# Experts chosen first, two of four routers as fp32 dots on VectorE, a softmax in two halves, and first outputs moved among the operand sums

## Chip, cores and metric

The kernel runs on one core of a Trainium2 chip. The metric is device time of one execution in microseconds, median of several runs.

## Reference, cut to what matters

```python
# x: [4, 512, 512]; layer 1: layernorm, an int8-quantised gated MLP per batch, residual
x = x + xattn(_layernorm(x), gate_up, ctx)
# layer 2, on the 2048 tokens xn = _layernorm(x):
logits = xn @ gate_w.T                            # gate_w: [8, 512]
_, sel = top_k(logits.sum(axis=0), 2)             # two experts for all tokens
rw = softmax(logits[:, sel], axis=1)              # a weight per token and expert
h = gelu(einsum('nd,kdf->knf', xn, w1[sel]) + b1[sel][:, None, :])
y = einsum('knf,kfd->knd', h, w2[sel]) + b2[sel][:, None, :]
out = x + einsum('nk,knd->nd', rw, y)
```

The same two experts serve all tokens. The softmax is over two logits only, so a weight depends on their difference alone.

## The kernel before, in words

It is a Bass program written by engine: each engine has a list of calls in its own order, and semaphores tie them together. PE is TensorE, DVE VectorE, ACT ScalarE, POOL GpSimd, SP the engine that issues the loads.

*Layer 1* (to about 140 us) runs the four batches b = 0 to 3 interleaved. *Layer 2* takes the two experts in 16 units of 256 hidden columns, 8 "pairs" of two halves: half tp = 0 has batches 0 and 1, tp = 1 batches 2 and 3. Every fp32 operand is split into a high part (rounded, made on ACT) and a low part (the rest, made by a subtraction), and a product is three matmuls: high x high, high x low, low x high. `keep_hi`/`keep_lo(b, h)` make those of the normalised, transposed tokens of batch b; `hid_lo` (POOL) those of the hidden h; `first_weights` and `first_down_weights` those of the first w1 and w2 (ACT high, DVE low).

The head of layer 2 is the stretch in question:
- `normed2(b, h)` on PE transposes normalised tokens (L656). DVE and ACT sum them over tokens (`token_sums`, `token_total`); `expert_sums` on PE (L677) turns the sums into eight expert totals; `choose_experts` on DVE finds the top two (L1349) and SP then loads w1, w2 and bias rows of the chosen experts.
- `router(b)` on PE (L667) makes the logits of 512 tokens for all 8 experts, 8 matmuls with 512 columns each. ACT copies them out, `logit_columns(b)` (L685) transposes them back, and `pick_logits` on DVE picks the columns of the chosen two. POOL raises e to the (negative) difference (L523), and `token_weights` on DVE makes the softmax weights (L1519 to L1523).
- `first_pair` differs from later pairs: `plain(q, n)` (L850) computes four tiles of a half, 12 matmuls each, with plain products; from pair 1 on `strassen` (L792) needs seven products of combined operands instead of eight. The sums of operands that this wants are made during the first pair: `last_operands`, `middle_operands`, `fourth_operand` (L1295, L1310), their high parts `operand_hi` on ACT, low parts `operand_lo` on DVE (L1316).
- `down` (L805) multiplies h by w2 into four PSUM banks of y. `outputs_of(p, tp, s)` on DVE (L1541) adds weight times y to the residual in SBUF and thereby frees each bank (`y_free`), which the block of downs after the next waits for. `bias_rows` (L1532) adds b2. In later pairs `combine` (L1570) sums products on DVE; the next product into the same bank waits for it (`comb_ready`).

The order around the change is the order of the calls in each engine's list. DVE's first pair before, in short:

```python
last_operands(0); fourth_operand(0); token_weights()
outputs_of(0, 0, 0); middle_operands(0, 3); middle_operands(0, 4); outputs_of(0, 0, 1)
operand_lo(0, 0..3); last_operands(1); fourth_operand(1)
bias_rows(0); outputs(0, 1)
```

Of the kernel before, what the change touches and what calls it, by code (L numbers as in the profile page):

```python
# [5 lines left out]
ALU = mybir.AluOpType  # L6
# [5 lines left out]
AX = mybir.AxisListType  # L12
ds = bass.ds

P = 128
# [8 lines left out]
def xattn_ffn(  # L24
# [21 lines left out]
    NT = B * TT  # L46
    FW = 2 * P
# [14 lines left out]
    with ExitStack() as ctx:  # L62
# [6 lines left out]
        def each(name):  # L69
# [42 lines left out]
        logits = sb("logits", [2 * E, B, T])  # L112
# [8 lines left out]
        lk = sb("lk", [P, TOPK, NT])  # L121
        lmin = sb("lmin", [P, NT])
        lmax = sb("lmax", [P, NT])
# [12 lines left out]


# [16 lines left out]
        rstd = [batch_sb(f"rstd{c}_", [P, TT]) for c in (1, 2)]  # L154
        nmean = [batch_sb(f"nmean{c}_", [P, TT]) for c in (1, 2)]
# [78 lines left out]
        raw1_load, raw2_load = sem("raw1_load"), sem("raw2_load")  # L234
        b1_load, b2_load = sem("b1_load"), sem("b2_load")
# [18 lines left out]
        def _(sp):  # L254
# [37 lines left out]
            load_w1(0)  # L292
# [25 lines left out]
        def _(pool):  # L318
# [200 lines left out]
            def first_pair():  # L519
                hid_lo(0, 0, 0)  # L520
                hid_lo(0, 0, 1)
                pool.wait_ge(lsub_ready, 1)
                g.tensor_tensor(lpow[:, :], euler[:, :], lsub[:, :], ALU.pow).then_inc(lexp_ready, 1)  # L523
                hid_lo(0, 0, 2)
                hid_lo(0, 0, 3)
                weight_sums(0)
                for i in range(4):
                    hid_lo(0, 1, i)
                for i in range(7):
                    weight_lo(0, i)  # L530
                down_lo(0, 0, 1)
                down_lo(0, 1, 0)

            first_pair()
# [6 lines left out]
        def _(pe):  # L541
# [139 lines left out]
            def logit_columns(b):  # L681
                emptied(f"r.{b}")
# [156 lines left out]
            def plain(q, n):  # L839
# [3 lines left out]
                for h in range(KD // H):  # L843
                    if q == 0:
                        pe.wait_ge(a_ops_ready, 2 * f + h + 1)
# [780 lines left out]
```

## Time and profile before

| what | value |
|---|---|
| time, median of 3 runs (lowest, highest) | 819.7 us (818.9, 820.05) |
| profiled execution, span from first to last instruction | 818.7 us |
| its own time as shown | the span alone is given for it; the median of the runs is 1.0 us above the span |
| PE busy | 771.5 us (94%) |
| DVE busy | 477.7 us (58%) |
| POOL busy | 449.7 us (55%) |
| ACT busy | 354.6 us (43%) |
| first tile of layer 2 (L850) on PE | from about 153.6 us on |

A busy PE says that its queue is full, not that its clock is: the granted clock is read apart. Shares over the whole span hide that DVE is much fuller in the first pair than later.

### The profile page before, as it was taken

Reading aid. Unit: us, or ns where it says so; the run is one execution under the profiler, and the core shown is the slowest. Engines: PE = TensorE matmul, PEld = TensorE weight load, DVE = VectorE, ACT = ScalarE, POOL = GpSimd, SP = SyncE. Lnnn points to the kernel's source line nnn. Section 1 sums busy time; section 2 is a strip of 40 time slices with the busy share of each in tenths; the row PEclk is TensorE's granted clock in tenths of the full one; section 3 lists DMA queues with packets and bytes.
Section 4 is the critical chain, followed back from the end, with each engine's and each line's share of the span. In section 5 each row is a group of like instructions: output and inputs, shape, how many; then the busy total and the mean of one; then the engine's idle time right before and its main releaser. Section 6 shows DMA issues by size and latency. Waiting matters only on the chain.

```text
span 818.7 us, 11342 instructions
## 1 busy us (share of the span) xinstructions
PE 771.5 (94%) x3570; PEld 624.1 (76%) x3577; DVE 477.7 (58%) x669; ACT 354.6 (43%) x660; POOL 449.7 (55%) x497
## 2 busy tenths in 40 slices
PE   5688666999999999999999999999999999999998
PEld 4666455688788888888888888888888888888886
DVE  5999759797754545454545454545454545454545
ACT  3967588743442434343424343434343434242422
POOL 1789997157564646464646464646464646464622
PEclk9899968999999999999999999999999999999999
DMA  9400000301010101010101010101010101010022
GB/s 344 173 2 1 1 0 2 129 1 51 1 52 1 51 0 49 3 50 2 48 4 51 1 45 6 42 9 44 7 41 11 36 15 36 15 32 19 0 103 104
DMA packets 19077, 32.34 MB, mean 39 GB/s; under 512 B 872, under 2 KB 11240, under 8 KB 18160
## 3 DMA queue, kind: packets, MB, share of 16 engines
q1 hardware_dynamic: 18896, 31.98, 11.1%
q8 instruction: 12, 0.20, 0.1%
q10 hardware_dynamic: 160, 0.08, 0.0%
q14 instruction: 9, 0.07, 0.0%
HBM read 27.87 MB, written 4.19 MB: 39 GB/s over the span
## 4 chain that ended last, share of the span: by engine, by line
PE 83%; POOL 8%; DVE 3%; issue 2%; ACT 2%; DMA 1%; ACTq 0%; POOLq 0%; DVEq 0%
PE slot L805 42%; PE slot L792 34%; PE slot L850 3%; POOL wv L366 2%; POOL xf L383 1%; PE slot L667 1%; POOL wv L372 1%; POOL cv L366 1%; PE slot L585 1%; DVE rmax L1226 1%; DMA b_rows<-in_L_ffn_b 1%; POOL rstd L340 1%; POOL h_lo L476 1%; DVE stats L1217 1%; DVE peak_x L1226 1%
## 5 line engine op out<-in xcount | busy, mean ns | idle before, releaser
L792 PE MATMUL slot<-xo,a_hi 128*128 128x512 f32 x840 | 259.1, 390 | 0.0
L1541 DVE SCALAR_TENSOR_TENSOR res<-slot,rw,res 128x512 f32<-128x512 f32 x256 | 178.5, 750 | 130.3 <-PE slot L805 130.2
L1570 DVE TENSOR_TENSOR e<-slot,e 128x512 f32<-128x512 f32 x150 | 103.8, 692 | 173.4 <-PE slot L792 173.3
L805 PE MATMUL slot<-w_hi,h_hi 128*128 128x512 f32 x512 | 201.3, 393 | 0.4 <-POOL h_lo L476 0.4
L805 PE MATMUL slot<-w_lo,h_hi 128*128 128x512 f32 x512 | 199.6, 390 | 0.0
L805 PE MATMUL slot<-w_hi,h_lo 128*128 128x512 f32 x512 | 199.4, 390 | 0.0
L792 PEld LDWEIGHTS slot<-xo,a_hi 128*128 128x128 f32 x840 | 157.4, 188 | 33.3 <-DVE e L1570 0.2
L476 POOL TENSOR_TENSOR h_lo<-e,h_hi 128x512 fp32r<-128x512 f32 x96 | 138.1, 1451 | 55.0 <-ACT e L1104 54.0
L792 PE MATMUL slot<-xo,a_lo 128*128 128x512 f32 x420 | 163.7, 390 | 0.0
L805 PEld LDWEIGHTS slot<-w_hi,h_hi 128*128 128x128 f32 x512 | 96.1, 188 | 25.1 <-POOL h_lo L476 5.6
L476 POOL TENSOR_TENSOR h_lo<-hid,h_hi 128x512 fp32r<-128x512 f32 x32 | 44.1, 1378 | 124.7 <-ACT hid L1104 124.7
L805 PEld LDWEIGHTS slot<-w_hi,h_lo 128*128 128x128 f32 x512 | 96.2, 188 | 20.1
L805 PEld LDWEIGHTS slot<-w_lo,h_hi 128*128 128x128 f32 x512 | 96.2, 188 | 19.3
L792 PEld LDWEIGHTS slot<-xo,a_lo 128*128 128x128 f32 x420 | 78.9, 188 | 16.5
L1103 ACT ACTIVATE h_hi<-e,b_now 128x512 fp32r<-128x512 f32 x90 | 64.9, 721 | 58.0 <-DVE e L1570 57.6
L1142 ACT COPY e<-slot 128x512 f32<-128x512 f32 x30 | 17.6, 587 | 164.5 <-PE slot L792 164.5
L490 POOL TENSOR_TENSOR a_lo<-raw,a_hi 128x256 fp32r<-128x256 f32 x45 | 34.3, 761 | 95.9 <-ACT a_hi L988 95.9
L991 ACT CAST w_hi<-raw 128x512 fp32r<-128x512 f32 x32 | 19.8, 622 | 109.8 <-PE slot L805 109.8
L495 POOL TENSOR_TENSOR w_lo<-raw,w_hi 128x512 fp32r<-128x512 f32 x30 | 38.7, 1289 | 50.4 <-ACT w_hi L991 50.4
L1104 ACT ACTIVATE e<-e,b_now 128x512 f32<-128x512 f32 x90 | 63.8, 709 | 0.0
L1103 ACT ACTIVATE h_hi<-slot,b_now 128x512 fp32r<-128x512 f32 x38 | 26.2, 689 | 66.5 <-PE slot L792 56.6
L490 POOL TENSOR_TENSOR a_lo<-ssum,a_hi 128x256 fp32r<-128x256 f32 x60 | 43.7, 739 | 0.0
(145 smaller groups left out, 814.5 us busy)
## 6 DMA issues: line engine op xcount, KB each, us to landing
raw<-in_L_ffn_w SPq DMA_DIRECT2D x32, 512.0 KB, 3.4
res<-in_x SPq DMA_DIRECT2D x4, 1024.0 KB, 11.9
wv<-in_fside_BxS2xS SPq DMA_DIRECT2D x4, 1024.0 KB, 12.8
out_x<-res SPq DMA_DIRECT2D x3, 1024.0 KB, 3.9
cv<-in_ctx SPq DMA_DIRECT2D x4, 512.0 KB, 13.1
out_x<-res SPq DMA_DIRECT2D x4, 256.0 KB, 2.7
b_row<-in_L_ffn_b SPq DMA_DIRECT2D x2, 256.0 KB, 4.6
b_rows<-in_L_ffn_b ACTq DMA_DIRECT2D x1, 64.0 KB, 6.0
```

The source lines that it names most:

```text
L366: g.tensor_tensor(w[:, j, :], w[:, j, :], rows[b][:, 0:n], ALU.mult).then_inc(wmul_ready[b], 1)
L476: g.tensor_tensor(h_lo[:, i, :], hid[i][:, :], h_hi[:, i, :].bitcast(F32), ALU.subtract).then_inc(h_ready, 1)
L490: g.tensor_tensor(a_lo[:, i, :, :], A_OF[i], a_hi[:, i, :, :].bitcast(F32), ALU.subtract).then_inc(a_ops_ready, 1)
L495: g.tensor_tensor(w2_lo[:, f, :], raw2[:, f, :], w2_hi[:, f, :].bitcast(F32), ALU.subtract).then_inc(w2_ready, 1)
L792: last = t.matmul(dst, a[:, i, k, :], xo[tp][:, v, k, :], start=(start and n == 0), stop=(n == 3 * H - 1), skip_group_check=True)
L805: last = t.matmul(y_bank[j][:, :], a[:, i, j * P:(j + 1) * P], v[:, f, :], start=(start and n == 0), stop=(not start and n == 2), skip_gro ...
L850: last = t.matmul(TILE_BANK[n], a[:, 2 * f + h, k, :], xo[q][:, v, k, :], start=(m == 0), stop=(m == 3 * KD - 1))
L991: s.copy(w2_hi[:, f, :], raw2[:, f, :]).then_inc(w2_hi_ready, 1)
L1103: s.activation(h_hi[:, i, :], src, ACT.Gelu_apprx_tanh, bias=bias).then_inc(hid_ready, 1)
L1104: s.activation(hid[i][:, :], src, ACT.Gelu_apprx_tanh, bias=bias).then_inc(hid_ready, 1)
L1541: v.scalar_tensor_tensor(out=r, in0=y_bank[j][:, :], scalar=rw[:, ds(p, 1), n:n + 1].rearrange("p a b -> p (a b)"), in1=r, op0=ALU.mult, o ...
L1570: v.tensor_tensor(dst[:, :], src, other[:, :], ALU.add).then_inc(comb_ready, 1)
```

## The change

It makes these edits:
- DVE and PE choose the experts earlier: `expert_sums` stands ahead of all routers, `keep_lo(0, 0)` and `keep_lo(0, 1)` stand behind `choose_experts`, `normalise_last` ahead of `keep_lo(1, 0)`; picking the experts and their b1 stands ahead of `first_weights`.
- The first w1 load is split in two halves, and the first tile's low-part matmuls come behind the high-part ones of the same half of K.
- Routers of batches 2 and 3 are gone from PE, and their copies and transposes. Two gate rows are loaded after w2, POOL subtracts them (`gate_difference`), and DVE makes eight dots of residual rows with the difference (`router_dots`).
- The softmax is made in two halves (`token_power`, `logit_maxima`, `token_weights`, each per tp).
- DVE's first pair is written in another order; on ACT `first_down_weights` and `keep_hi(3, 1)` stand behind the first gelu and `operand_hi` between the gelus of the second half.

```diff
+            first = w1_v[ds(expert[0], 1), 0].rearrange("e p k f -> (e p) k f")
+            sp.dma_start(raw1[:, 0:H, :], first[:, 0:H, :]).then_inc(raw1_top, 16)
+            sp.dma_start(raw1[:, H:KD, :], first[:, H:KD, :]).then_inc(raw1_load, 16)
             load_w2(0)
             expert.append(value_of(1))
+            for k in range(TOPK):
+                sp.dma_start(gate_row[:, k, :], gate_w[ds(expert[k], 1), :].to_broadcast([P, D])).then_inc(gate_load, 16)
...
+            def gate_difference():
+                pool.wait_ge(gate_load, 16 * TOPK)
+                g.tensor_tensor(gate_row[:, 0, :], gate_row[:, 0, :], gate_row[:, 1, :], ALU.subtract
+                                ).then_inc(gate_ready, 1)
+            token_power(0)
+            gate_difference()
+            hid_lo(0, 0, 0)
...
+            expert_sums()
             router(1)
-            expert_sums()
             router(0)
-            router(2)
-            router(3)
...
+            def router_dots(b):
+                dve.wait_ge(nmr_ready[b], 2)
+                dve.wait_ge(gate_ready, 1)
+                for j in range(TT):
+                    n = b * TT + j
+                    product = part(1, (T2L, T4L)[j // 2])[:, (j % 2) * D:(j % 2) * D + D]
+                    ins = v.scalar_tensor_tensor(out=product, in0=res[:, n, :], scalar=nmean[1][b][:, j:j + 1],
+                                                 in1=gate_row[:, 0, :], op0=ALU.add, op1=ALU.mult,
+                                                 accum_out=ldot[:, n:n + 1])
+                link(ins)
+                link(v.tensor_tensor(ldiff[:, b * TT:b * TT + TT], ldot[:, b * TT:b * TT + TT], rstd[1][b][:, :],
+                                     ALU.mult))
...
+            normalise_last()
             keep_lo(1, 0)
-            normalise_last()
             token_sums(2)
-            keep_lo(1, 1)
             token_sums(3)
             token_total()
+            keep_lo(1, 1)
+            choose_experts()
+            keep_lo(0, 0)
             keep_lo(0, 1)
...
+            token_weights(0)
+            first_down_weights()
+            router_dots(2)
+            keep_lo(3, 0)
+            last_operands(0)
+            outputs_of(0, 0, 0)
+            keep_lo(3, 1)
+            fourth_operand(0)
+            outputs_of(0, 0, 1)
+            middle_operands(0, 3)
+            middle_operands(0, 4)
+            router_dots(3)
+            logit_maxima(1)
+            operand_lo(0, 0)
+            operand_lo(0, 1)
+            token_weights(1)
+            operand_lo(0, 2)
+            operand_lo(0, 3)
+            outputs_of(0, 1, 0)
+            last_operands(1)
+            outputs_of(0, 1, 1)
+            fourth_operand(1)
+            dve.wait_ge(b2_load, 16 * TOPK)
+            bias_rows(0)
```

On PE, between the last transposes and the first tile, this stood before (16x512 and 8x512 rows are the routers, 128x8 the expert sums; semaphores are named):

```order
L667 MATMUL slot<-xo,gwt 16x512 [waits lo_ready1,drained2]
...
L677 MATMUL slot<-gwt_full,tok_total 128x8 [waits drained3,tok_ready]
L677 MATMUL slot<-gwt_full,tok_total 128x8 x3
L667 MATMUL slot<-xo,gwt 16x512 [waits lo_ready0,drained0]
...
L667 MATMUL slot<-xo,gwt 16x512 [waits lo_ready2,drained3]
...
L667 MATMUL slot<-xo,gwt 16x512 [waits lo_ready3,drained1]
```

and of the change this stands at the same place:

```order
L698 MATMUL slot<-gwt_full,tok_total 128x8 [waits drained3,tok_ready]
L698 MATMUL slot<-gwt_full,tok_total 128x8 x3
L688 MATMUL slot<-xo,gwt 16x512 [waits lo_ready1,drained0]
...
L688 MATMUL slot<-xo,gwt 16x512 [waits lo_ready0,drained2]
```

The expert sums moved ahead of the routers, and two of four routers are gone.

On DVE, this stood before between the pick of the logits and the second block of outputs (L1295 and L1310 are the operand sums, L1541 the outputs):

```order
L1366 TENSOR_TENSOR lsub<-lmin,lmax 128x16
L1367 TENSOR_TENSOR is_top<-lk 128x16
L1368 TENSOR_TENSOR is_top<-lk 128x16
L1295 TENSOR_TENSOR xf<-xf 128x1024 x2
L1310 TENSOR_TENSOR xf<-xf 128x1024
L1519 TENSOR_TENSOR lexp<-lpow,is_top 128x16 x2
L1520 TENSOR_SCALAR lden<-lpow 128x16
L1521 RECIPROCAL lrec<-lden 128x16
L1523 TENSOR_TENSOR rw<-lexp,lrec 128x128 x2
L1541 SCALAR_TENSOR_TENSOR res<-slot,rw,res 128x512 x4
L1295 TENSOR_TENSOR xf<-xf 128x1024 x2
L1541 SCALAR_TENSOR_TENSOR res<-slot,rw,res 128x512 x4
```

and of the change (L1404 are the dots, L1332 keep_lo, L1444 the low parts of w2, L1336 operand sums, L1597 the outputs):

```order
L1424 TENSOR_SCALAR is_top<-ldiff 128x8
L1332 TENSOR_TENSOR xo<-xf,xo 128x1024
L1574 TENSOR_TENSOR lexp<-lpow,is_top 128x8 x2
...
L1444 TENSOR_TENSOR w_lo<-raw,w_hi 128x512 x2
L1404 SCALAR_TENSOR_TENSOR xf,ldot<-res,late_nmean,gate_row 128x512 x4
L1408 TENSOR_TENSOR ldiff<-ldot,late_rstd 128x4
L1332 TENSOR_TENSOR xo<-xf,xo 128x1024
L1336 TENSOR_TENSOR xf<-xf 128x1024 x2
L1597 SCALAR_TENSOR_TENSOR res<-slot,rw,res 128x512 x4
L1332 TENSOR_TENSOR xo<-xf,xo 128x1024
L1351 TENSOR_TENSOR xf<-xf 128x1024
L1597 SCALAR_TENSOR_TENSOR res<-slot,rw,res 128x512 x4
```

The first outputs now follow the low parts of w2, four dots, a keep_lo and two operand sums.

Still on DVE, the end of the first pair stood so before (L1316 are operand_lo, L1532 bias rows):

```order
L1316 TENSOR_TENSOR xo<-xf,xo 128x1024 x4
L1295 TENSOR_TENSOR xf<-xf 128x1024 x2
L1310 TENSOR_TENSOR xf<-xf 128x1024
L1532 SCALAR_TENSOR_TENSOR res<-b_row,rw,res 128x512 x2
```

with eight outputs behind it, and of the change so (L1357 is operand_lo, L1351 fourth_operand, L1588 bias rows):

```order
L1357 TENSOR_TENSOR xo<-xf,xo 128x1024 x2
L1597 SCALAR_TENSOR_TENSOR res<-slot,rw,res 128x512 x4
L1336 TENSOR_TENSOR xf<-xf 128x1024 x2
L1597 SCALAR_TENSOR_TENSOR res<-slot,rw,res 128x512 x4
L1351 TENSOR_TENSOR xf<-xf 128x1024
L1588 SCALAR_TENSOR_TENSOR res<-b_row,rw,res 128x512 x2
```

The fourth operand and the bias rows moved from ahead of the last outputs to behind them.

## Rows read from the trace of the kernel before

**Rows 1.** The page: busy us, share of the span and instructions of each engine

```profile
PE 771.5 (94%) x3570; PEld 624.1 (76%) x3577; DVE 477.7 (58%) x669; ACT 354.6 (43%) x660; POOL 449.7 (55%) x497
```

**Rows 2.** Timeline of PE from 139.5 us: start, length, engine, instruction, count, [idle before]

```profile
139.89 3.87 PE L656 MATMUL slot<-ident,xf 128*128 128x128 f32 x16 [0.81 <-ACT xf L895]
143.41 3.14 PE L667 MATMUL slot<-xo,gwt 128*16 128x512 f32 x8
146.38 0.95 PE L677 MATMUL slot<-gwt_full,tok_total 128*128 128x8 f32 x8
147.19 6.52 PE L667 MATMUL slot<-xo,gwt 128*16 128x512 f32 x24
...
159.11 1.17 PE L685 MATMUL slot<-ident,logits 16*128 16x16 f32 x16
```

**Rows 3.** Chain that ended last, 150 to 300 us: start, length

```profile
165.97 10.88 PE slot L805 x48
```

**Rows 4.** Waits of PE from 154 us to the end: us, times, longest

```profile
PE slot L805 <- POOL h_lo L476: 0.4, 1, 0.4
```

**Rows 5.** Windows: PE, PEld, DVE, ACT, POOL busy, granted clock, DMA share, GB/s

```profile
136.00:142.00 6.00, 5.09 (x21) 3.96 (x22) 5.91 (x6) 3.55 (x7) 2.82 (x3) 0.50 0.00 1
...
144.00:146.00 2.00, 2.00 (x7) 0.70 (x6) 1.87 (x3) 2.00 (x3) 0.00 (x0) 0.58 0.00 0
...
156.10:201.40 45.30, 45.30 (x212) 37.41 (x211) 37.44 (x49) 19.08 (x34) 29.67 (x22) 1.00 0.09 30
```

**Rows 6.** Timeline of DVE from 135.9 us

```profile
135.98 2.86 DVE L1291 TENSOR_TENSOR xo<-xf,xo 128x1024 fp32r<-128x1024 f32 x2
...
143.79 1.23 DVE L1334 TENSOR_REDUCE tok_sum<-slot 128x2 f32<-128x1024 f32 x1 [1.59 <-PE slot L656]
...
147.86 0.16 DVE L1349 FIND_INDEX8 top_i<-top_v,sum_row 128x8 uint32<-128x8 f32 x1
147.94 4.61 DVE L1291 TENSOR_TENSOR xo<-xf,xo 128x1024 fp32r<-128x1024 f32 x4
```

**Rows 7.** Timelines of SP and ACT: the w1 load, its first cast

```profile
148.99 0.39 SPq L285 DMA_DIRECT2D raw<-in_L_ffn_w  x1
...
152.16 1.33 ACT L985 CAST a_hi<-raw 128x256 fp32r<-128x256 f32 x4 [1.87 <-DMA raw<-in_L_ffn_w]
```

**Rows 8.** Timeline of POOL: powers and low parts of h

```profile
125.40 1.03 POOL L340 TENSOR_TENSOR rstd<-var_e,neg_half 128x4 f32<-128x4 f32 x1 [0.18 <-DVE var_e L1223]
...
136.60 1.97 POOL L340 TENSOR_TENSOR rstd<-var_e,neg_half 128x4 f32<-128x4 f32 x1
...
158.46 1.27 POOL L476 TENSOR_TENSOR h_lo<-hid,h_hi 128x512 fp32r<-128x512 f32 x1 [19.56 <-ACT hid L1104]
...
162.69 2.90 POOL L523 TENSOR_TENSOR lpow<-euler,lsub 128x16 f32<-128x16 f32 x1 [0.84 <-DVE lsub L1366]
165.56 3.43 POOL L476 TENSOR_TENSOR h_lo<-e,h_hi 128x512 fp32r<-128x512 f32 x2
...
184.74 6.21 POOL L476 TENSOR_TENSOR h_lo<-e,h_hi 128x512 fp32r<-128x512 f32 x3
```

**Rows 9.** Timeline of DVE from 166 us

```profile
166.60 1.24 DVE L1519 TENSOR_TENSOR lexp<-lpow,is_top 128x16 f32<-128x16 f32 x2
167.76 1.26 DVE L1520 TENSOR_SCALAR lden<-lpow 128x16 f32<-128x16 f32 x1
...
170.07 2.73 DVE L1541 SCALAR_TENSOR_TENSOR res<-slot,rw,res 128x512 f32<-128x512 f32 x4
...
188.13 3.37 DVE L1532 SCALAR_TENSOR_TENSOR res<-b_row,rw,res 128x512 f32<-128x512 f32 x2
...
196.61 2.79 DVE L1541 SCALAR_TENSOR_TENSOR res<-slot,rw,res 128x512 f32<-128x512 f32 x4 [2.34 <-PE slot L805]
201.36 0.69 DVE L1570 TENSOR_TENSOR e<-slot,e 128x512 f32<-128x512 f32 x1 [1.97 <-PE slot L792]
...
271.05 0.76 DVE L1532 SCALAR_TENSOR_TENSOR res<-b_row,rw,res 128x512 f32 x1
```

More of the change, by code:

```diff
@@ L135, in xattn_ffn @@
         b1_now = sb("b1_now", [P, 2])
+        late_rstd = [sb(f"late_rstd{b}", [P, TT]) for b in range(B)]
+        late_nmean = [sb(f"late_nmean{b}", [P, TT]) for b in range(B)]
         early = ExitStack()
@@ L881, in _, with first_downs @@
-            first_pair()
+                if n == 3:
+                    pe.wait_ge(hid_ready, 8 + 8 * tp + 2)
+                if tp == 0 and n == 0:
+                    pe.wait_ge(drained[0], ALL_DRAINED[0])
+                if tp == 0 and n == 2:
+                    pe.wait_ge(drained[1], ALL_DRAINED[1])
+                plain(tp, n)
+            def first_downs(tp):
+                if tp == 0:
+                    pe.wait_ge(w2_ready, 2)
+                    pe.wait_ge(drained[2], ALL_DRAINED[2])
+                    pe.wait_ge(drained[3], ALL_DRAINED[3])
+                down(0, tp, 0, 0, 0, True)
+                down(0, tp, 0, 1, 1, False)
+                last = down(0, tp, 1, 2, 1, True)
+                if tp == 1:
+                    last.then_inc(w2_free, 1)
+                down(0, tp, 1, 3, 0, False)
@@ L882, in _ @@
+            up_tile(0, 0)
+            logit_columns(1)
+            logit_columns(0)
+            up_tile(0, 1)
+            up_tile(0, 2)
+            up_tile(0, 3)
+            first_downs(0)
+            for n in range(4):
+                up_tile(1, n)
+            first_downs(1)
+            pe.wait_ge(hid_ready, 8 + 16)
             pair(1, True, False)
@@ L1173, in pair @@
                         down_hi(0)
-            first_pair()
+            first_bias()
+            gelu_tile(0, 0)
+            first_down_weights()
+            keep_hi(3, 1)
+            gelu_tile(0, 1)
+            gelu_tile(0, 2)
+            gelu_tile(0, 3)
+            gelu_tile(1, 0)
+            operand_hi(0, (T2H, T2L), 4)
+            gelu_tile(1, 1)
+            operand_hi(0, (T3H, T3L), 4)
+            operand_hi(0, (T1H, T1L), 4)
+            gelu_tile(1, 2)
+            operand_hi(0, (T4H, T4L), 4)
+            gelu_tile(1, 3)
+            later_weights()
             pair(1, True, False)
@@ new lines, in pick_logits @@
+            def pick_logits():
+                dve.wait_ge(logcol_ps, 2)
+                cols = bank[3][:, 0:NT * E].rearrange("p (n e) -> p n e", e=2 * E)
+                link(v.tensor_tensor(between[:, :], onehot[:, 0, :], onehot[:, 1, :], ALU.subtract))
+                link(v.tensor_tensor(picked[:, 0:NT // 2, :], cols,
+                                     between[:, :].unsqueeze(1).to_broadcast([P, NT // 2, 2 * E]), ALU.mult))
+                link(v.tensor_reduce(ldiff[:, 0:NT // 2], picked[:, 0:NT // 2, :], AX.X, ALU.add))
@@ L1370, in pick_bias, with logit_maxima @@
+            def logit_maxima(tp):
+                at = slice(tp * HALF, tp * HALF + HALF)
+                v.scalar_tensor_tensor(out=lsub[:, at], in0=ldiff[:, at], scalar=-1.0, in1=ldiff[:, at],
+                                       op0=ALU.mult, op1=ALU.min).then_inc(lsub_ready, 1)
+                v.tensor_scalar(is_top[:, 0, at], ldiff[:, at], 0.0, None, ALU.is_ge)
+                link(v.tensor_scalar(is_top[:, 1, at], ldiff[:, at], 0.0, None, ALU.is_le))
             def pick_bias():
@@ L1547, in outputs @@
                 outputs_of(p, tp, 1)
-            def first_pair():
-                last_operands(0)
-                fourth_operand(0)
-                token_weights()
-                outputs_of(0, 0, 0)
-                middle_operands(0, 3)
-                middle_operands(0, 4)
-                outputs_of(0, 0, 1)
-                for n in range(4):
-                    operand_lo(0, n)
-                last_operands(1)
-                fourth_operand(1)
-                dve.wait_ge(b2_load, 16 * TOPK)
-                bias_rows(0)
-                outputs(0, 1)
             def pair(p, first, final):
```

157 lines of the change are left out of this document (63 added, 94 removed), and 8 rows, old and new, of the table SLOT_USES.

## The prediction, on record before the changed kernel ran

> **What bounds the kernel now.** The page first: PE is busy for 771.5 of 818.7 us [rows 1]. Then PE's own waits from 154 us to the end: one, of 0.4 us [rows 4]. So from the first expert matmul (L850) on, PE runs without a hole, and the time is (when L850 starts) + (PE's work behind it) + (holes). L850 starts behind the last of 24 router matmul records that begin at 147.19 and take 6.52 [rows 2], so at about 153.55. A matmul of 512 columns takes 0.227 in a row there (48 in 10.88 [rows 3]), so a tile of four is 10.9 and a block of 24 down matmuls 5.45. VectorE is the engine to watch beside it: between 156.1 and 201.4 it is busy for 37.4 of 45.3 us [rows 5], the rest are waits for PE, such as 2.34 before an output block and 1.97 before the first combine of pair 1 [rows 9]. That is its whole reserve in the stretch into which the change puts work.
>
> A second thing to see is how VectorE and GpSimd get in each other's way. A 128x16 TENSOR_SCALAR (L1520) took 1.26 us at 167.76 [rows 9], while GpSimd ran two low parts of h, 3.43 us from 165.56 on [rows 8]. Two bias rows took 3.37 [rows 9] beside three low parts that took 6.21 [rows 8]; alone a bias row takes 0.76 [rows 9] and a low part 1.27 [rows 8]. So these operations, with both operands in SBUF, take turns: one waits until the other has ended. Output updates, which read PSUM, don't: 2.73 for four at 170.07 [rows 9], beside GpSimd's weight sums.
>
> **What the change gives at the start.** (a) keep_lo(0,0) no longer stands in front of normalise_last. Before, it and keep_lo(1,0) took 2.86 from 135.98 [rows 6], and GpSimd's power at 136.60 took 1.97 where the same one took 1.03 at 125.40 [rows 8]. 0.95 is saved; normalised tokens come that much earlier, and PE's 0.81 hole at 139.89 [rows 2] goes. Last token sum (143.79, 1.23 us [rows 6]) and total: 0.8 to 1.1 earlier, at 144.1 to 144.4. (b) The expert sums stood behind router(1), at 146.38 [rows 2]; now they start when the total is there, take 0.95, and the choice, 0.7 behind them (147.33 to 148.02), is made at 145.9 instead of 148.02 [rows 6]: 2.1 earlier. (c) The w1 load is issued 0.97 after the choice, and the first weight is cast 3.17 after the issue [rows 7]. The first half is taken at 2.6 (an estimate: the 3.17 less a third for half the bytes, between 2.0 and 3.17), so the weight is ready for PE at 149.9. Routers 1 and 0 are through by 149.1 at full clock. First tile at 149.9 instead of 153.55: **3.6 earlier**. (d) 8 logit transposes instead of 16, of 1.17 us [rows 2]: **0.55**. Removing routers 2 and 3 (about 3.6 at full clock) is inside (c), since PE would wait for the weight anyway. The gate rows' loads go behind w2, land about 8 us behind the choice (around 154), and are wanted at 156: hidden, with 2 us to spare; they hold GpSimd's whole queue if they are late. Splitting the w1 load costs SP one issue of 0.39 [rows 7], not on the path. Together PE is **4.2 us** ahead when it has the four tiles of the first half: downs could start at 161.6 instead of 165.8.
>
> **What it puts on VectorE.** Behind the choice now stand six keep_lo instead of four (4.61 for four [rows 6], so +2.3), eight fp32 dots and two small scalings. No dot is in the trace. It is a scalar_tensor_tensor of 128x512 with both tensors in SBUF, as a bias row (0.76), with a sum beside it; an output update takes 0.68 in a row. I take 0.72 each, 2.9 for four, with bounds 0.62 and 1.07 (half as much again). Two token_weights instead of one. Against it about 1 us less of picking. About 8.5 us more in all against a reserve of 7.9, before taking turns is counted. I walk it through, in the new clock.
>
> 1. *Weights of the first half.* Logits of tokens 0 and 1 are picked at 154.3. GpSimd's power of 16 columns took 2.90 and of 4 columns 1.03 [rows 8], so 8 take 1.65: 156.0. Then gate_difference (1.25, as a low part of h) is in front: VectorE waits for it, 157.25. token_weights takes 3.4 as before (166.60 to 170.0 [rows 9]; every small step in it waits for a low part), and w_lo waits for one more low part (1.25) and takes 1.25: 163.1. Before, w_lo was done ahead of all this. PE wanted it at 161.6: **hole of 1.5**. It is gone if the power takes 1.0 and one turn is saved.
> 2. *Outputs of the first half.* Four dots to 166.0; low part 1.25, scaling 0.2 and a weight sum of 0.7 on GpSimd: 168.15; keep_lo(3,0) 1.15; two last_operands 2.45 with a sum of 0.7 between: 172.4; first bank of y free at 173.1. PE is through with the first 24 down matmuls 5.45 behind 163.1, at 168.55, and wants that bank: **4.6**. Without GpSimd's turns (2.65) it is 1.9.
> 3. *The second half.* Outputs end 175.1. keep_lo(3,1), fourth_operand, four outputs, middle_operands: 182.7. Dots 185.6. Two low parts of h (2.5): the first gelu result of this half is there at 181, and VectorE's unbroken row has kept GpSimd out: 188.3 with the small steps. Two low operands 2.3, token_weights with its two low parts 3.3, a weight part 0.7, two low operands 2.3: 196.9; first bank free 197.6. PE is at 173.3 + 5.45 + 10.9 + 5.45 = 195.0: **2.6**.
> 4. *Into pair 1.* last_operands now lie between the two output blocks, in the place of the 2.34 wait [rows 9], and fourth_operand and the bias rows lie behind them: outputs to 199.6, operands with two turns 202.8, outputs 205.5, one turn, fourth_operand 1.2 and bias rows 1.6: 208.9. Pair 1 starts on PE at 203.1, and the first combine could start 2.9 later (two products of six matmuls and 0.2), at 206.0. So it is 2.9 late, and the two middle_operands and the next combine hang on it: **3.5** of holes (2.5 in front of the fourth product, 1.0 in front of the sixth).
>
> Holes 12.2, less 4.2, is +8.0. The same bookkeeping with the same durations, walked through the kernel before, brings its first combine at 202.1 and not at 201.36: 0.75 too late, so it overcharges turns. **I take +7** on the span of 818.7; the runs' median, 819.7, is 1.0 above the profiled span, which I add as it stands. Forecast: 819.7 + 7 = 826.7, put at 826.5.
>
> Bounds: with dots at 0.62, 1 us less; at 1.07, 2.8 more. With the fewest turns (holes of 0.3, 1.9, 0.5 and 2.5): 5.2 - 4.2 = +1.0, 820.7.
>
> **A rule that speaks against the dots.** The bias row [rows 9] reads two fp32 tensors from SBUF at 0.76, no slower than an update from PSUM, but it has no running sum. The Trainium skill (Vector Engine (DVE) Microarchitecture Reference, Points that are easy to get wrong) says that a scalar-tensor-tensor with two non-bf16 SBUF sources runs at half throughput, since no read port is left for the accumulator. By that the eight dots would take about 0.55 us more each; no dot is in this trace to test it.
>
> **Rivals.**
> A. *VectorE keeps up, and the kernel is faster.* For it: the reserve of 7.9 nearly covers the added 8.5; and GpSimd could do its low parts under the output updates, which don't take turns. Against it: the low parts come due at 155 to 166, when VectorE has no update to do. Without any turn the walk leaves only the wait for w1 and gives 3.3 less than before: **816.4**. It decides by whether the first output update of pair 0 starts before 168. Chance 0.13.
> B. *The clock comes back late.* The granted clock was 0.50 from 136 to 142 and in 144 to 146 it was 0.58 on the mean [rows 5]: it rose at 145.6 after PE had worked without a hole since 139.89, with router(1) at 0.39 a matmul [rows 2]. Now PE stands still for a microsecond or more ahead of the expert sums. If it stays at 1.2 GHz through the expert sums (an estimated 0.6 more) and the 16 router matmuls (0.43 instead of 0.23 each, begun at 145.2), the first tile starts at 152.7 and all else 2.8 later: **829**. Against it: closing the 0.81 hole could raise it earlier, at 142. Chance 0.2.
> C. *The dots take half as long again or more* (1.07): eight times 0.35, **829.3**. Chance 0.12.
> D. *Even:* fewest turns, or smaller holes in steps 3 and 4: 819 to 821. Chance 0.07.
> The forecast has the remaining 0.48.
>
> **How the numbers follow.** 0.2% (1.6 us) is about what a measurement of this kernel can tell from no change. Slower: forecast, B and C, 0.80. Within 0.2%: D, 0.06. Faster: A and a sliver of D, 0.14. The range leaves out A (816.4) and goes from 820, just below the fewest-turns bound, to 830.5, above B and C alone; B and C together (832) are left out.
>
> **What would show it.** Expert sums ahead of the routers and the choice near 146; the first L850-like matmul near 150 (152.7 by B). On VectorE no waits for PE between 157 and 200, small operations of over 1 us, and dots near 0.72. On PE four holes: in front of the first down for w_lo, in front of the third of the four down blocks of each half for VectorE's updates (the largest in the first half), and in front of the fourth product of pair 1 for a combine. From pair 2 on the two traces should run alike, shifted by the result. It is wrong if PE has no holes near 168 and 195, if the dots don't take turns with GpSimd, or if the choice is not earlier.

## The result, and the profile after

| | before | after |
|---|---|---|
| median (lowest, highest), runs of one chip | 819.3 us (818.55, 820.05) | 830.26 us (829.88, 830.51) |
| profiled span | 818.7 us | 828.7 us |

The ratio is 1.0127, 95% interval 1.011 to 1.0144: slower by 10.4 us by the ratio and by 11.0 by the medians. The prediction said 826.5 us, between 820.0 and 830.5, and slower with 0.8: the sign is right, and the time lies in the range, 0.2 us under its upper end.

The page of the changed kernel, busy us, share and instructions:

```profile
PE 772.7 (93%) x3553; PEld 622.0 (75%) x3553; DVE 491.8 (59%) x693; ACT 353.3 (43%) x658; POOL 450.0 (54%) x499
```

Set beside [rows 1], PE's busy time is 1.2 us longer although 3.6 us of router matmuls are gone; part of it ran at the lower clock. VectorE has 14.1 us more. The span hides where: the timeline of PE from 139 us on has these starts that had waited (start, length, [idle before <- releaser]):

```profile
143.10 1.06 PE L698 MATMUL slot<-gwt_full,tok_total 128*128 128x8 f32 x8 [1.62 <-DVE tok_total L1383]
...
162.18 0.50 PE L825 MATMUL slot<-w_hi,h_hi 128*128 128x512 f32 x1 [1.02 <-DVE w_lo L1444]
...
172.47 0.77 PE L825 MATMUL slot<-w_hi,h_hi 128*128 128x512 f32 x1 [4.52 <-DVE res L1597]
...
199.43 0.47 PE L825 MATMUL slot<-w_hi,h_hi 128*128 128x512 f32 x1 [2.19 <-DVE res L1597]
...
210.58 0.73 PE L812 MATMUL slot<-xo,a_hi 128*128 128x512 f32 x2 [1.39 <-DVE e L1610]
...
214.67 0.73 PE L812 MATMUL slot<-xo,a_hi 128*128 128x512 f32 x2 [1.08 <-DVE e L1610]
```

[rows 4] had one wait of 0.4 us, which is still there. From the first expert matmul on there are five more (the last five of the lines above), 10.2 us together, all for VectorE; the prediction's fourth hole, of two parts, is two of them. Up to there the change had won what it could: the expert sums start at 143.10 instead of 146.38 [rows 2], and PE was ready for the downs at 161.16 (162.18 less 1.02), where before they began at 165.81: 4.65 us ahead.

Windows of the changed kernel (us; PE, PEld, DVE, ACT, POOL busy; granted clock; DMA share; GB/s):

```profile
155.00:212.00 57.00, 47.88 (x196) 38.15 (x195) 53.56 (x71) 19.04 (x33) 30.67 (x25) 0.94 0.09 30
168.00:172.00 4.00, 0.00 (x0) 0.00 (x0) 3.93 (x4) 0.00 (x0) 0.07 (x1) 0.93 0.00 0
172.00:178.00 6.00, 5.53 (x13) 4.45 (x14) 4.57 (x6) 0.00 (x0) 0.00 (x0) 0.50 0.00 0
```

VectorE is busy for 53.6 of 57 us, against 47.2 in the same stretch before. PE is idle through the second window, and in the third it is granted 0.50, that is 1.2 GHz, for the first 6 us after the hole; its down matmuls there follow each other at 0.43 us instead of 0.227.

The timeline of VectorE shows what "busy" is made of:

```profile
155.77 1.32 DVE L1574 TENSOR_TENSOR lexp<-lpow,is_top 128x8 f32<-128x8 f32 x2 [0.33 <-POOL lpow L538]
157.01 1.26 DVE L1575 TENSOR_SCALAR lden<-lpow 128x8 f32<-128x8 f32 x1
158.31 0.20 DVE L1576 RECIPROCAL lrec<-lden 128x8 f32<-128x8 f32 x1
...
162.05 0.74 DVE L1404 SCALAR_TENSOR_TENSOR xf<-res,late_nmean,gate_row 128x512 f32<-128x512 f32 x1
162.72 0.07 DVE L1404 DVE_READ_ACCUMULATOR xf<-res,late_nmean,gate_row 128x1 f32 x1
162.72 1.77 DVE L1404 SCALAR_TENSOR_TENSOR xf<-res,late_nmean,gate_row 128x512 f32<-128x512 f32 x1
...
164.43 1.21 DVE L1404 SCALAR_TENSOR_TENSOR xf<-res,late_nmean,gate_row 128x512 f32<-128x512 f32 x1
...
165.57 1.21 DVE L1404 SCALAR_TENSOR_TENSOR xf<-res,late_nmean,gate_row 128x512 f32<-128x512 f32 x1
...
171.58 2.73 DVE L1597 SCALAR_TENSOR_TENSOR res<-slot,rw,res 128x512 f32<-128x512 f32 x4
...
178.95 2.76 DVE L1597 SCALAR_TENSOR_TENSOR res<-slot,rw,res 128x512 f32<-128x512 f32 x4 [2.38 <-PE slot L825]
...
209.84 0.69 DVE L1610 TENSOR_TENSOR e<-slot,e 128x512 f32<-128x512 f32 x1
210.45 3.45 DVE L1336 TENSOR_TENSOR xf<-xf 128x1024 f32<-128x1024 f32 x2
```

Eight numbers a partition took 1.26 us at 157.01. The same dot took 0.74, then 1.77, then 1.21 twice. GpSimd's timeline names the partners: the difference of the gate rows beside the first line, a low part of h beside the 1.26 and the 1.77, and sums of weights (`ssum`) beside the two of 1.21:

```profile
155.70 1.29 POOL L532 TENSOR_TENSOR gate_row<-gate_row 128x512 f32<-128x512 f32 x1
156.96 1.30 POOL L487 TENSOR_TENSOR h_lo<-hid,h_hi 128x512 fp32r<-128x512 f32 x1
158.21 1.29 POOL L487 TENSOR_TENSOR h_lo<-e,h_hi 128x512 fp32r<-128x512 f32 x1
...
162.54 1.41 POOL L487 TENSOR_TENSOR h_lo<-e,h_hi 128x512 fp32r<-128x512 f32 x1 [0.96 <-ACT e L1132]
163.91 1.19 POOL L492 TENSOR_TENSOR ssum<-raw 128x256 f32<-128x256 f32 x1
165.17 1.06 POOL L494 TENSOR_TENSOR ssum<-ssum,raw 128x256 f32<-128x256 f32 x1
```

The result closes on VectorE's list. The first combine of pair 1 starts at 209.84 instead of 201.36 [rows 9], 8.5 us later. The two middle_operands behind it take 3.45 us (taking turns) where the kernel before had 2.48, another 1.0. The last combine of pair 1 starts at 238.88 and started at 229.41, 9.5 later. The spans differ by 10.0: PE has no wait for another engine behind that point in either trace, and the last 0.5 I can't place.

### The profile page after: what moved, and what is told of

It is laid out like the page before. It is cut to its first block, busy times and chain, and to the rows that moved or that the text cites. A ratio compares the mean times of both kernels' runs of the same rounds, so it can differ in the third digit from the quotient of the medians.

```text
span 828.7 us, 11336 instructions
## 1 busy us (share of the span) xinstructions
PE 772.7 (93%) x3553; PEld 622.0 (75%) x3553; DVE 491.8 (59%) x693; ACT 353.3 (43%) x658; POOL 450.0 (54%) x499
## 4 chain that ended last, share of the span: by engine, by line
PE 77%; DVE 9%; POOL 8%; issue 3%; ACT 1%; DMA 1%; SPq 0%; ACTq 0%; DVEq 0%; POOLq 0%
PE slot L825 40%; PE slot L812 33%; POOL wv L377 2%; POOL xf L394 1%; DVE xf L1404 1%; DVE peak_x L1267 1%; PE slot L606 1%; POOL wv L383 1%; DVE res L1597 1%; POOL cv L377 1%; DVE rmax L1267 1%; DMA b_rows<-in_L_ffn_b 1%; POOL h_lo L487 1%; DVE xo L1357 1%; PE slot L677 1%
## 5 line engine op out<-in xcount | busy, mean ns | idle before, releaser
L1597 DVE SCALAR_TENSOR_TENSOR res<-slot,rw,res 128x512 f32<-128x512 f32 x256 | 178.7, 750 | 130.4 <-PE slot L825 130.4
L487 POOL TENSOR_TENSOR h_lo<-e,h_hi 128x512 fp32r<-128x512 f32 x96 | 136.2, 1431 | 58.8 <-ACT e L1132 57.8
```

What stands on the lines that cost most here:

```text
L487: g.tensor_tensor(h_lo[:, i, :], hid[i][:, :], h_hi[:, i, :].bitcast(F32), ALU.subtract).then_inc(h_ready, 1)
L1597: v.scalar_tensor_tensor(out=r, in0=y_bank[j][:, :], scalar=rw[:, ds(p, 1), n:n + 1].rearrange("p a b -> p (a b)"), in1=r, op0=ALU.mult, o ...
```

## The experiments

Theory V is the one that the first runs test: in the first pair VectorE's list, stretched by turns with GpSimd, is the bound, and PE's holes only show where it happens to be late. All runs are paired with the kernel before on the same chip (819.95 us for the first four, 820.2 for the next four, 821.7 for the next two, 820.04 for the last). The change itself was not run again beside them, and its own pair had 819.3. So a step from the change to a variant is known from medians to 1 or 2 us only, and where it is that small the trace has to decide.

**Outputs earlier.** The change, with the first output block ahead of a keep_lo and two operand sums:

```diff
+            outputs_of(0, 0, 0)
             keep_lo(3, 0)
             last_operands(0)
-            outputs_of(0, 0, 0)
```

> The change, with the first four outputs ahead of keep_lo(3,0) and last_operands(0). Theory V (VectorE is the bound of the whole first pair, holes of PE only show it): PE's 4.5 us hole shrinks to under 1 and the clock doesn't fall in it, but VectorE has only its one wait of 2.4 us to give back, so a later hole grows (2.2 to 5 or more) and the time falls by 2 to 3, to about 828. Theory L (each hole is local, made by what stands ahead of it): 4.5 and the 3.0 of the clock come back, 822.8.

829.59 us, ratio 1.0104 [1.0074, 1.0134]. PE's waits:

```profile
169.43 0.47 PE L825 MATMUL slot<-w_hi,h_hi 128*128 128x512 f32 x1 [0.40 <-DVE res L1597]
...
197.69 0.77 PE L825 MATMUL slot<-w_hi,h_hi 128*128 128x512 f32 x1 [6.24 <-DVE res L1597]
```

The hole of 4.52 shrank to 0.40 and the next grew from 2.19 to 6.24: 6.64 instead of 6.71. The order only moves the lateness. Theory L, at 822.8, falls. V had the sign and the shape, but it also gave 2 to 3 us back, and the profiled span is 828.9, none better than 828.7: VectorE's wait of 2.38 for PE did not go, it came back as one of 2.21 ahead of a later output block, since PE was late there. So the holes are not to be costed one by one.

**Clock kept up.** The change, with matmuls without use in front of the downs that wait:

```diff
+                if tp == 0:
+                    pe.wait_ge(lsub_ready, 1)
+                    for _ in range(18):
+                        t.matmul(bank[3], w2_hi[:, 0, 0:P], w2_hi[:, 1, :], start=True, stop=True,
+                                 skip_group_check=True)
```

> The change, with 18 idle matmuls of 512 columns (their result is used by nobody) on PE ahead of the third block of downs, where its 4.5 us hole lies. Theory C (the clock fell because of the hole, and cost 3.0 us): the granted clock stays at 1.0, the block that took 8.2 takes 5.4; VectorE's wait of 2.4 at 179 goes, and the time falls by 2.4 to 3.0, to 827.5. If the clock costs nothing since VectorE is late anyway: 830.3. If it fell for another reason, it is at 0.5 again from 172 to 178.

829.35 us, 1.0103 [1.0073, 1.0132]. The clock did stay up (the window, as above):

```profile
172.00:178.00 6.00, 5.57 (x25) 4.54 (x25) 5.96 (x8) 0.00 (x0) 0.00 (x0) 1.00 0.00 0
```

and 25 matmuls ran where 13 had. Yet the time is only 0.9 us lower by the medians (2.0 by the ratios, within the two intervals), the profiled span 0.6 (828.1), and VectorE reached the first combine of pair 1 at 209.41 instead of 209.84. What PE won went later:

```profile
197.65 0.77 PE L825 MATMUL slot<-w_hi,h_hi 128*128 128x512 f32 x1 [3.06 <-DVE res L1602]
```

This hole is 0.9 longer than the change's 2.19 at the same place, and behind it the granted clock fell in its turn (0.66 from 197 to 199, 0.50 from 199 to 201), where in the change it had stayed at 1.00. So the run did not keep the clock up throughout; it shows that the 3 us of the first fall were not to be had for themselves, since VectorE was late whatever PE did.

**Short dots.** The change with dots over 64 of 512 columns, so the weights of batches 2 and 3 are not the reference's:

```diff
-                    ins = v.scalar_tensor_tensor(out=product, in0=res[:, n, :], scalar=nmean[1][b][:, j:j + 1],
-                                                 in1=gate_row[:, 0, :], op0=ALU.add, op1=ALU.mult,
+                    ins = v.scalar_tensor_tensor(out=product, in0=res[:, n, 0:64], scalar=nmean[1][b][:, j:j + 1],
+                                                 in1=gate_row[:, 0, 0:64], op0=ALU.add, op1=ALU.mult,
```

> The change, with dots over 64 of the 512 columns (logits of the second half are then not those of the model). Theory V: eight times 0.58 is 4.6 off VectorE, some turns with it and the clock's fall if the hole gets short: 822 to 825. Theory L: only the hole in front of the third block of downs shrinks, by 2.3 (four dots), and the clock's 3.0 may come back: 825 to 828. If dots don't matter: 830.3.

827.21 us, 1.0081 [1.0053, 1.011]: a dot takes 0.27 us, its mean had been 1.12, so 6.8 us of dots went (eight times 0.85) and the time fell by 3.05 (the profiled span by 4.4). That is outside V's 822 to 825 and inside L's 825 to 828, and the holes look like L too: the second shrank from 4.52 to 2.23, the others hardly changed (0.84, 2.18, 1.39, 1.08). Only 4.0 us of the 6.8 reached the first combine (205.84): VectorE now waited for others, 1.27 for PE, 0.77 for ACT and 1.54 for GpSimd's second power. VectorE's list by itself is therefore not the whole bound. The turns stayed: lden still took 1.26, and the scaling behind the dots 1.13 where it had taken 0.57.

**No low parts in GpSimd's hands.** The change, with the first pair's low parts of h set to zero (those products lack them). The zeroing reads nothing:

```diff
-            hid_lo(0, 0, 0)
+            def no_lo(p, tp, i):
+                pool.wait_ge(hid_ready, 8 + 8 * (2 * p + tp) + 2 * i + 2)
+                g.memset(h_lo[:, i, :].bitcast(F32), 0.0).then_inc(h_ready, 1)
+            no_lo(0, 0, 0)
```

and so for all eight.

> The change, with the low parts of h of the first pair set to zero by a memset on GpSimd instead of a subtraction (the low x high products of that pair are then left out). A memset reads no SBUF. Theory T (taking turns makes the holes): VectorE's small operations and dots fall back to their own lengths, 8 turns of about 1.0 go, and the time falls to 820 to 823. If turns are no matter: 829 to 830.3.

820.53 us, 1.0007 [0.9993, 1.0021]. VectorE, the same lines as above:

```profile
157.25 0.47 DVE L1579 TENSOR_SCALAR lden<-lpow 128x8 f32<-128x8 f32 x1
...
159.60 0.75 DVE L1408 SCALAR_TENSOR_TENSOR xf<-res,late_nmean,gate_row 128x512 f32<-128x512 f32 x1
...
200.34 0.69 DVE L1614 TENSOR_TENSOR e<-slot,e 128x512 f32<-128x512 f32 x1
```

All eight dots take 0.75; the first combine of pair 1 comes at 200.34, 9.5 us earlier, with every dot in place, and VectorE is busy for 482.6 us instead of 491.8. With the dots at their own length and these turns gone, the loss is gone. That GpSimd's list got shorter too is no rival: in the change VectorE waited for it once, for 0.33 us, and PE once, for 0.4, and with the memsets such waits are no shorter (0.34 and 0.41 for VectorE, 0.41 for PE). But the added work isn't free without these turns. Three holes are left (1.12, 1.39 and 1.07), the operand sums still take turns with the sums of weights (3.44 for two at 163.75, where 2.47 is their own), and they use up the start: the downs begin at 161.39, 4.4 us ahead of before, and the kernel is no faster. The Trainium skill (SBUF — State Buffer, Who interferes with whom) has this rule: an instruction of VectorE with two SBUF inputs blocks against one of GpSimd that reads SBUF, not against one that only writes it. This pair of runs agrees: beside GpSimd's reads a dot took up to 1.78 us, beside memsets of 0.53 us each always 0.75.

**The control.** It has the same memsets in the kernel before (the same work left out).

> The kernel before, with GpSimd's low parts of h in the first pair set to zero by a memset instead of a subtraction (this work is left out, so those products lack it): the control of the run in which the same was done to the change. Theory V: the kernel before has no hole in this stretch, VectorE just gets more waits for PE, the time stays (0 to -0.4 us, PE's one wait of 0.4 for h_lo). Rival (the memset itself makes the time less by something else than turns, for example a shorter PE or a later stage): the time falls by several us as it did in the change, towards 810.

820.29 us, 1.0007 [0.9995, 1.0019]: no gain. Before the change the same turns cost nothing, since VectorE's waits for PE covered them; freed of them, VectorE only waits longer in front of output blocks:

```profile
169.76 2.73 DVE L1545 SCALAR_TENSOR_TENSOR res<-slot,rw,res 128x512 f32<-128x512 f32 x4 [1.70 <-PE slot L809]
...
191.52 2.73 DVE L1545 SCALAR_TENSOR_TENSOR res<-slot,rw,res 128x512 f32<-128x512 f32 x4 [3.82 <-PE slot L809]
...
196.90 2.79 DVE L1545 SCALAR_TENSOR_TENSOR res<-slot,rw,res 128x512 f32<-128x512 f32 x4 [2.65 <-PE slot L809]
```

**The end of the pair alone.** The kernel before with the change's tail, shown against its old one:

```diff
+                outputs_of(0, 1, 0)
                 last_operands(1)
+                outputs_of(0, 1, 1)
                 fourth_operand(1)
                 bias_rows(0)
-                outputs(0, 1)
```

> The kernel before, with one part of the change alone: the end of VectorE's first pair in the change's order (outputs of tp 1 step 0, last_operands(1), outputs step 1, fourth_operand(1), bias rows). Theory V (VectorE's list has no room behind its only wait): fourth_operand and the bias rows now lie behind the last outputs, VectorE comes 1.4 to 2 us late into pair 1, PE gets one hole in front of the fourth product: 820.8 to 821.5, +1.5 to +2.5 in the paired comparison with the span's. Rival (the two operand sums fill the 2.34 us wait and all is absorbed): no hole, no difference, within 0.3 us.

824.13 us, 1.005 [1.0034, 1.0067], more than expected. PE's timeline:

```profile
205.15 0.73 PE L792 MATMUL slot<-xo,a_hi 128*128 128x512 f32 x2 [1.39 <-DVE e L1571]
...
209.24 0.73 PE L792 MATMUL slot<-xo,a_hi 128*128 128x512 f32 x2 [1.08 <-DVE e L1571]
```

The two holes are those of the change to the hundredth, 2.5 us, of the 3.9 us by which the medians differ. Another 1.1 of the profile's 4.2 stands ahead of the downs (first one at 166.88, before 165.81), where nothing was edited; the last 0.6 I can't place. So layer 1 can come out a microsecond apart between kernels that are written alike there, and differences of that size in one profile prove little.

**The start alone.** The kernel before with experts first, w1 in halves, high products first; two routers on PE stand behind the first tile instead of ahead of it:

```diff
-            router(2)
-            router(3)
...
+                    if tp == 0:
+                        router(2)
+                        router(3)
```

> The kernel before with the change's start alone: experts chosen ahead of all routers, w1 in two halves, high products first; all four routers stay on PE (two of them behind the first tile), VectorE's first pair in the order of before. Router matmuls that stood ahead of the first tile (3.6 us) now stand behind it, so PE's work is the same and only its idle time at the start can shrink. Theory V: PE idle was 0.8 us before the transposes and no more, so -0.5 to -2 us, no hole later, 818 to 819.3. Rival (the start gives the full 4.2 us by itself, the loss is all VectorE's): 815.5. Rival (clock comes late): +0 to +2.

820.88 us, 1.0006 [0.9995, 1.0017]: nothing, where I had expected 0.5 to 2 us. The first tile starts at 149.71, 3.8 us earlier, but the two routers are still to be done behind it, and PE has new waits, 1.62 for the total and 1.10 for the weight (0.79 and 0.31). The clock wasn't late (granted 1.00 from 141 on):

```profile
143.76 1.06 PE L680 MATMUL slot<-gwt_full,tok_total 128*128 128x8 f32 x8 [1.62 <-DVE tok_total L1351]
144.67 4.24 PE L670 MATMUL slot<-xo,gwt 128*16 128x512 f32 x16
149.71 1.16 PE L853 MATMUL slot<-xo,a_hi 128*128 128x512 f32 x4 [0.79 <-ACT a_hi L991]
```

The downs start at 166.30, 0.5 later than before. So the earlier choice by itself gives nothing: the change's 4.65 us need the matmuls and transposes taken off PE as well. The other half alone, routers taken off and the choice left late, was not run. By the rows of before it could not give the whole either: the first cast of w1 started at 152.16 [rows 7] and the first tile at 153.55, so without routers PE would have waited there for the weight.

**One router of four as dots.** The kernel of the start alone, with batch 3's router as four dots in VectorE's wait for the logits, one softmax:

```diff
+            router_dots(3)
```

> The one before plus one router of four (batch 3) as four dots on VectorE, placed where VectorE had waited 2.4 us for the logits, with a single softmax for all batches. PE loses 8 matmuls of 512 columns (1.8 us) and some transposes. Theory V: 3 us of dots fit only partly into the wait; a hole of some 0.5 to 1 us in front of the downs and one behind it, net -1.3 to -2 us against before, 817.5 to 818.5. Rival (any dots in this stretch collide with GpSimd's low parts and cost more than PE saves): +1 to +3 us.

825.78 us, 1.0073 [1.0059, 1.0086]: I expected a gain, it lost 5.6. PE was at the downs at 163.41, 2.4 ahead of before, and then:

```profile
173.76 0.77 PE L815 MATMUL slot<-w_hi,h_hi 128*128 128x512 f32 x1 [4.74 <-DVE res L1570]
```

Two of the four dots took 1.78 and 1.77. All behind them came late, and a hole of 4.74 followed, with the lower clock behind it (granted 0.50 from 173 to 179). This was the rival, at about twice its price. Nothing is left out here and the tail is that of before, so the loss comes without the change's other parts; that it is half of the change's 11 us for half of the dots proves no proportion.

**Softmax on GpSimd.** Everything is computed; the weights are made by a second power, so that VectorE loses its longest row of turns. GpSimd's part:

```diff
+            def token_weights(tp):
+                at = slice(tp * HALF, tp * HALF + HALF)
+                link(g.tensor_tensor(lrec[:, at], lden[:, at], minus[:, at], ALU.pow))
+                q = lrec[:, at].unsqueeze(1).to_broadcast([P, EP, HALF])
+                g.tensor_scalar(rw[:, EP:2 * EP, at], q, 1.0, None, ALU.mult).then_inc(lexp_ready, 1)
+                g.tensor_scalar(rw[:, 0:EP, at], q, -1.0, 1.0, ALU.mult, ALU.add).then_inc(lexp_ready, 1)
```

> The change with the softmax weights made by GpSimd alone: after the power, GpSimd adds 1, raises to -1 and writes both weights (it had nothing to do from 168 to 185 us); VectorE loses both token_weights and the maxima (3.98 us from 155.77, 3.5 us from 191.78, 0.5 us twice), each step of which had waited for a low part of h. Nothing is left out. Theory V (VectorE's list with its turns is the bound in the first pair): VectorE is 4 us earlier at the first outputs and 7 to 8 us at the end of the pair; the holes of 1.0 and 4.5 us go or shrink to below 1.5 together, the clock stays up, the hole of 2.2 goes; the two holes in pair 1 (2.5 together) stay at least in part, since the tail's order is kept: 819 to 822. Rival G (GpSimd's list becomes late instead, its power of -1 and the writes take 2.5 us in front of the weight sums and low parts): PE waits for weights or for low parts, 824 or more.

827.48 us, 1.0081 [1.0063, 1.01]. V had expected 819 to 822, rival G 824 or more. VectorE lost about 8 us of work and came to the first combine only 2.2 us earlier:

```profile
159.15 1.69 DVE L1416 SCALAR_TENSOR_TENSOR xf<-res,late_nmean,gate_row 128x512 f32<-128x512 f32 x1 [2.04 <-POOL gate_row L534]
...
160.78 1.77 DVE L1416 SCALAR_TENSOR_TENSOR xf<-res,late_nmean,gate_row 128x512 f32<-128x512 f32 x1
...
195.59 2.73 DVE L1591 SCALAR_TENSOR_TENSOR res<-slot,rw,res 128x512 f32<-128x512 f32 x4 [4.77 <-POOL rw L548]
...
207.62 0.69 DVE L1604 TENSOR_TENSOR e<-slot,e 128x512 f32<-128x512 f32 x1
```

The power took 2.55 instead of 1.64 (beside a keep_lo), the gate rows came late, then all of the first four dots took turns, 1.69 to 1.77, and VectorE waited 4.77 for the second weights. So of about 8 us moved from VectorE to GpSimd 2.8 came back (830.26 to 827.48; 3.8 by the ratios). V in its first form, VectorE's list alone, falls here: both lists count. That they act as one resource is not shown. GpSimd stood idle for 9.58 us before the second half's low parts, and the second weights stand behind all four of those in its list; an order with the weights ahead of the last two was not run.

**The tail put back**, twice: in the run above, and in the run with memsets.

```diff
-            outputs_of(0, 1, 0)
             last_operands(1)
-            outputs_of(0, 1, 1)
             fourth_operand(1)
             bias_rows(0)
+            outputs_of(0, 1, 0)
+            outputs_of(0, 1, 1)
```

> The one before, with the end of VectorE's first pair in the order of the kernel before (operand sums and bias rows ahead of both output blocks). Theory V: if VectorE now has about 2 us of room ahead of the outputs of the second half, the two holes of pair 1 (1.4 and 1.1) go and nothing takes their place: 1 to 2.5 us under the run above, 816.5 to 819.5, under the kernel before by what PE lost in router matmuls less the holes that are left. Rival (VectorE still has no room): a hole of 1 to 3 us stands in front of the third block of downs of the second half instead, no gain over the run above.

> The run memset_lo (the change with the first pair's low parts of h set to zero, so those products lack it), with the end of VectorE's first pair in the order of the kernel before. In memset_lo PE had four holes left: 1.12 in front of the third block of the first half and 1.39 and 1.07 in pair 1. Theory V (with no turns VectorE has room ahead of the outputs of the second half, where it waited 0.89 us for PE): fourth_operand and bias rows (2.7 us without turns) ahead of the outputs make at most 1.8 us of lateness there, the two holes of pair 1 go: net -0.7 to -2.5 us against memset_lo, 818 to 819.8, that is the first version faster than the kernel before by something that can be measured, though only with work left out. Rival (the two orders are worth the same whatever VectorE's room): 820.5, no difference.

828.56 us, 1.0094 [1.0075, 1.0112], and 825.99 us, 1.0077 [1.0055, 1.0098]. My expectation fell in both: the first is 1.1 worse than the run above (827.48) and not 1 to 2.5 better, the second not 0.7 to 2.5 better than 820.53 but 5.5 worse. PE's hole in the second:

```profile
195.98 0.76 PE L829 MATMUL slot<-w_hi,h_hi 128*128 128x512 f32 x1 [5.33 <-DVE res L1601]
```

In the kernel before, the change's tail costs 3.9 us (2.5 of them in holes); in the version with memsets the same tail saves 5.5. Operand sums and bias rows took 3.44, 1.63 and 2.22 there, 7.3 in all, in front of outputs ahead of which VectorE had 0.89 us of room; I had counted only the last two, and without turns. With pool_tail the sign is the same but the size is not: one hole of 4.84 in place of 2.10 and 2.09, and 1.1 us. The change itself with the tail of before was not run, so what its tail is worth there isn't measured.

## Why the prediction was right, and where it was off

**What bounds the kernel; the sign.** Right. VectorE's reserve (7.9) was smaller than what was added: its busy time rose by 14.1 us. The control shows the other side: with the reserve untouched, the same turns cost nothing. One sign failed: VectorE did wait once for PE in the stretch (2.38 at 178.95), as PE was at the lower clock. And there is luck in the range. Its upper end of 830.5 was set by rivals B and C, each alone, and neither is what made the time; the mechanism of the forecast did, with +11.0 us where +7 had been forecast.

**Start gain of 4.2.** 4.65 measured. The choice was made at 144.84 (predicted 145.9), since the token total was there at 143.05 and not at 144.1; the first half of w1 was cast at 148.43, 2.6 after its issue, as estimated. My reading that the removed routers were "inside (c)", and so worth nothing of their own, was half of it: choice_pe, which keeps them, starts its downs 0.5 later than before (tail_only shows 1.1 at that place with nothing edited ahead of it), so the earlier choice is worth nothing without their removal either.

**Dots at 0.72.** 0.74 alone, plus 0.07 for an instruction that reads the sum, nearly hidden. The rule of the Trainium skill that I had weighed (Vector Engine (DVE) Microarchitecture Reference, Points that are easy to get wrong) gives half throughput for such a dot. The measured 0.74 for 128x512 fp32 with a sum, against 0.76 for a bias row without one [rows 9], doesn't agree with it, and rival C's reason falls with it. The mean was nevertheless 1.12, 0.40 over my price where C had asked for 0.35: C's size came, by turns. The step that failed in the sum is "four dots to 166.0", which gave them 2.9 us. They took 4.7, three of the first four and one of the second four in turns that I had not given them; they ended at 166.79 only because they began a microsecond before the 163.1 of the walk. The softmax held (predicted behind a wait of 1.25 and 3.4 long, to 160.65; measured to 159.72, with that turn inside it), and so did w_lo's turn (2.5 predicted, 2.38).

**The holes: 1.5, 4.6, 2.6, 3.5.** Measured 1.0, 4.5, 2.2, 2.5, at the places named. Their sum, 10.2, is 2.0 smaller. 0.6 of that lies in the first two. The other 1.4 lies behind the clock's fall, where PE came later to the places at which VectorE is late; pe_filler agrees, for with the clock kept up the third grew by 0.9.

**The clock, missing.** 96 matmuls of 0.227 from 172.47 take 21.8 us, they took 24.8: 3.0 of lower clock behind the hole of 4.5. The holes and the start alone give 10.2 - 4.65 = 5.6; with 3.0 it is 8.6, and for the remaining 0.9 up to 9.5 the restarts behind holes are left, which the waits don't list (the matmul behind the first hole's first one comes after 0.34 us instead of 0.227); I have not summed them. The clock isn't a cost that adds to VectorE's lateness: with the first fall bridged, 0.9 comes back and not 3. Along VectorE's list the sum is simpler: the walk had the first combine at 208.9, which is 7.5 late; measured 209.84, 8.5 late; and 1.0 more for the turn in the middle_operands, which I left out.

**"I take +7."** This was the worst step. The walk gave 827.7; the 0.75 and two roundings took off 1.2. But the walk did not overcharge the changed kernel, it brought the first combine 0.9 too early. That it came out late for the kernel before is no bias that carries over; that VectorE's waits for PE swallow turns there, and not here, is my reading, which the control supports. With the walk's own +8.0 and that 1.0 the forecast would have been 828.7.

**The rivals.** A fell (first outputs at 171.58, not before 168). B: its condition came in part. The clock was up at 142 to 144 (1.00), then fell behind PE's wait of 1.62, to 0.53 in 144 to 146 and 0.61 in 146 to 148, and the 16 router matmuls took 5.42 us (4.24 in choice_pe, at 1.00). The first tile followed them without a wait at 149.28. It cost 0.4 at most, not 2.8, since the first weight was only ready at 148.84. C fell by its reason and not by its size (above). D fell: the turns came.

## What to carry

Where two engines take turns in a stretch, budget both lists: of about 8 us moved from one to the other 2.8 came back, and a run in which one list alone was shortened by 6.8 gave 3 to 4.4. Give the added work the measured length of its neighbours in that stretch, not its length alone (1.12 us against 0.74 here). An order is good or bad only for a given lateness: the tail that cost 3.9 us in the kernel before saved 5.5 in the version with memsets and 1.1 in the one with the weights on GpSimd, so price a reordering last, after the work that comes with it.

## What was not expected of the hardware

- A small operation with one SBUF input (TENSOR_SCALAR, 128x8) waited as long as those with two: 1.26 us beside a low part of h, 0.16 without a partner. The prediction had the same line of the kernel before [rows 9] but counted it among operations with both operands in SBUF. It was longer beside memsets too, which the dots weren't: in memset_lo it took 0.47 and 0.56 beside memsets of 0.53, and 0.17 in before_memset, where none ran beside it.
- A run of VectorE operations with two SBUF inputs without a pause kept GpSimd out for more than one operation: beside low operands of 1.15 each, a low part of h of 1.27 alone took 2.64 in tail_only (at 182.09) and 3.75 in the kernel before (at 181.02).
- How long a stay at 1.2 GHz a hole brings differs, and its length alone doesn't order it. Some 6 us at 0.50 followed the holes of 4.52 (the change), 4.74 (four_dots) and 6.24 (out_first); about 3 us followed those of 2.23 (short_dots), 3.06 (pe_filler), 3.42 (pool_weights: 0.59, 0.50, 0.50 and 0.70 in the four microseconds from 172 on), 4.84 (pool_tail) and 5.33 (memset_tail). None followed those of 1.12 (memset_lo: 1.00 from 168 to 175) and 2.19 (the change: 1.00 from 194 to 204). PE's wait of 1.62 for the token total was followed by a fall in the change and by none in choice_pe.
